# A gated linear-attention layer on one core: a new order at head and tail, gate's low part ahead of the masks, and a shorter reciprocal root with ScalarE's square

## What is computed

```python
xn = layernorm(x)                       # over the features, eps 1e-5
q, k, v = silu(xn @ Wq), silu(xn @ Wk), silu(xn @ Wv)
# per head, decay exp(ld): S_t = exp(ld) * S_{t-1} + k_t v_t^T ;  o_t = q_t S_t
gate = (xn @ Wg1) @ Wg2                 # 256 -> 16 -> 256
o = o * sigmoid(gate)
o = o * rsqrt(mean(o * o over the head's 16) + 1e-5) * norm_w
s = o @ Wo
g = silu(dequantised(fp8(xn * scale)) @ dequantised(fp8(W2 * scale1)))
out = x + s * g
```

## Time and profile before

| | us |
|---|---|
| median of 3 runs | 157.53 |
| lowest, highest | 156.8, 158.95 |
| the profiled execution's own time | 157.87 |
| its span, first to last instruction | 156.1 |
| busy in the span: PE, PEld, DVE, ACT, POOL | 131.1, 110.5, 109.1, 72.7, 73.2 |
| mean granted TensorE clock | 0.967 |

### The profile page before, as it was taken

How to read it: one execution, slowest core, us unless ns; L and a number is a source line. 1 busy time by engine, 2 the same in 40 slices (tenths; PEclk the granted TensorE clock), 3 DMA queues, 4 the chain that set the end, 5 groups by cost and what they waited for, 6 DMA issues and landing times.

```text
span 156.1 us, 7273 instructions
## 1 busy us (share of the span) xinstructions
PE 131.1 (84%) x3156; PEld 110.5 (71%) x3156; DVE 109.1 (70%) x302; ACT 72.7 (47%) x133; POOL 73.2 (47%) x112
## 2 busy tenths in 40 slices
PE   4987793793899997999799979897999798879781
PEld 4876692571798786779677967686878786668770
DVE  0766999654797589848984898289738961765854
ACT  3597570847466635573557355436541653001000
POOL 5758657594633366526652656166316630040030
PEclk9999999569689999999999999999999999999999
DMA  3988000000000000100100010000200020020003
GB/s 82 274 263 274 8 0 6 0 6 0 6 0 4 4 4 21 51 4 4 45 28 4 4 60 16 0 8 0 73 4 6 0 71 0 4 71 4 4 22 112
DMA packets 6847, 6.06 MB, mean 39 GB/s; under 512 B 1376, under 2 KB 6816, under 8 KB 6816
## 3 DMA queue, kind: packets, MB, share of 16 engines
q1 hardware_dynamic: 6816, 5.60, 11.3%
HBM read 3.50 MB, written 2.10 MB: 36 GB/s over the span
## 4 chain that ended last, share of the span: by engine, by line
PE 54%; DVE 26%; issue 10%; ACT 5%; DMA 2%; SPq 1%; DVEq 0%; ACTq 0%
PE b_q L1098 9%; PE b_o L1054 8%; PE b_o L1038 5%; PE b_v L917 3%; PE b_v L1104 3%; PE b_x L890 3%; DVE probs L641 3%; PE b_s L954 3%; PE b_k L980 3%; PE b_s L970 2%; DMA w_f<-in_L_attn_Wq_dram 2%; DVE b_x L688 2%; DVE b_x L686 2%; DVE sg L736 2%; PE b_v L920 2%
## 5 line engine op out<-in xcount | busy, mean ns | idle before, releaser
L333 POOL TENSOR_TENSOR e_sum<-e_y,e_magic 128x512 f32<-128x512 f32 x8 | 10.7, 1341 | 18.8 <-DVE e_magic L626 18.8
L674 DVE SCALAR_TENSOR_TENSOR og<-gate_tanh,b_o 128x512 f32<-128x512 f32 x8 | 5.5, 688 | 17.7 <-PE b_o L1054 17.7
L1054 PE MATMUL b_o<-probs,v_par 64*32 64x64 f32 x1024 | 15.9, 230 | 1.4 <-issue 1.4
L351 POOL TENSOR_TENSOR own_mid<-state_mid,head_parity 128x128 f32<-128x128 f32 x8 | 3.2, 401 | 26.8 <-DVE state_mid L654 22.5
L1054 PEld LDWEIGHTS b_o<-probs,v_par 64*32 64x32 f32 x1024 | 10.5, 110 | 7.1 <-issue 6.0
L341 POOL TENSOR_TENSOR qd<-q_silu,q_decay 128x512 f32<-128x512 f32 x8 | 10.3, 1293 | 9.8 <-ACT q_silu L468 9.8
L1098 PE MATMUL b_q<-wo_scaled,on 128*128 128x256 f32 x56 | 14.2, 394 | 0.8 <-DVE on L715 0.8
L369 POOL TENSOR_TENSOR y<-sg,x_sb 128x512 f32<-128x512 f32 x7 | 8.9, 1270 | 11.3 <-DVE sg L736 11.3
L917 PE MATMUL b_v<-w_hi,xT_hi 128*128 128x256 f32 x32 | 9.0, 302 | 5.2 <-DVE g1T L636 4.9
L468 ACT ACTIVATE q_silu<-b_q 128x512 f32<-128x512 f32 x8 | 4.8, 598 | 18.1 <-PE b_q L909 18.1
L1098 PEld LDWEIGHTS b_q<-wo_scaled,on 128*128 128x128 f32 x56 | 10.0, 189 | 2.7 <-DVE on L715 1.0
...
## 6 DMA issues: line engine op xcount, KB each, us to landing
...
```

The source lines that it names most:

```text
L333: g.tensor_tensor(e4_sum[:], e4_y[:, n % 2], e4_magic[:, n % 2], ALU.add).then_inc(s_e4sum, 1)
L674: v.scalar_tensor_tensor(out=og[:, n % 2], in0=gate_tanh[:, n % 2], scalar=1.0, in1=ps_o, op0=ALU.add, op1=ALU.mult).then_inc(s_og, 1)
L1054: mm = t.matmul(ps_o[32 * r:32 * r + 32, c, z:z + C], v_par[rows, u, blk:blk + 2 * E], probs[rows, r, s, i:i + C], start=(half == 0 and s ...
```

## The change

- **Loop.** `low_g1` comes ahead of the four masks.
- **Root.** A seed and Newton step with tuned constants (three operations), then a third-order step: two products and a last multiply on DVE and, between them, a square with a bias on ScalarE (`square_w`). `head_spread`'s factor takes up the constant 3/8. `square_w(n - 1)` stands on ScalarE ahead of `silu_q(n + 1)`.
- **Wg2.** The four loads go into a zeroed `wg2_f32` (they wait for the fill), and the stack is one cast and one multiply-add with a column that is -1 on the low rows and 0 elsewhere.
- **Head.** Wv is loaded ahead of the second x tiles; the first scale has its own semaphore. w_hi of Wq moves from ScalarE to DVE. GpSimd fills its constants ahead of the first `norm_factors`, does the second behind both selects of the decay mask, and `round_y(0)` ahead of `decay_q(0)` and the sum for W2. ScalarE scales y ahead of the second table load and finds the over-range values of step 0 earlier. DVE takes exponent and magic of step 0 ahead of the masks and the W2 steps behind them. TensorE transposes k of step 0 between the halves of v.
- **Tail.** DVE finishes the root of step 6 but for its pair before it gates step 7; four `keep_warm` calls ahead of the last o matmuls go, and others become fewer (14 to 12 at the start, 4 to 2 and 12 to 5 at the end).

```diff
@@ sync
             load_w(1, Wk)
+            sp.dma_start(scales[:, 0:1], scale.unsqueeze(0).broadcast_to([P, 1])).then_inc(s_scale[0], 16)
+            load_w(2, Wv)
             sp.dma_start(x_sb[:, x_tiles(1), :], x_v[:, x_tiles(1), :]).then_inc(s_x[1], 16)
-            load_w(2, Wv)
...
+            sp.wait_ge(s_pool, 15)
             for r in range(4):
                 sp.dma_start(wg2_f32[32 * r:32 * r + GR, :], Wg2).then_inc(s_wg2, 16)
@@ gpsimd
             pool.wait_ge(s_pool, 11)
-            norm_factors(0)
...
-            g.memset(wg2_stack[:].bitcast(F32), 0.0).then_inc(s_pool, 1)
+            g.memset(wg2_f32[:], 0.0).then_inc(s_pool, 1)
+            norm_factors(0)
+            g.memset(minus_53[:], -5.0 / 3.0)
+            g.memset(minus_third[:], 0.0).then_inc(s_pool, 1)
...
+            g.memset(minus_third[64:96], -1.0).then_inc(s_pool, 1)
...
-                if c == 0:
-                    pool.wait_ge(s_pool, 18)
-                    norm_factors(1)
-                    pool.wait_ge(s_shift, 2)
-            pool.wait_ge(s_pool, 19)
+            pool.wait_ge(s_pool, 21)
+            norm_factors(1)
             pool.wait_ge(s_dvec, 5)
             decay_k(0)
+            round_y(0)
+            decay_q(0)
             pool.wait_ge(s_w2q, 3)
             g.tensor_tensor(w2_m[:], w2_y[:], w2_f32[:], ALU.add).then_inc(s_w2sum, 1)
-            decay_q(0)
             norm_factors(2)
-            round_y(0)
@@ scalar
+            def square_w(n):
+                act.wait_ge(s_rs, RS_STEPS * n + 7)
+                a.activation(rs_half, rs_err, ACT.Square, bias=minus_53[:, 0:1]).then_inc(s_rs, 1)
...
-            high_w(0)
...
+            act.wait_ge(s_scale[0], 16)
+            scale_y(0)
             a.activation(table_load[:, 1:2], eps_col[:, 0:1], ACT.Silu)
             silu_k(0)
...
             normalise(1)
-            act.wait_ge(s_small, 32)
-            scale_y(0)
...
             silu_k(1)
+            find_over(0)
+            act.wait_ge(s_pool, 18)
+            silu_v(1)
             gate(0)
-            act.wait_ge(s_pool, 17)
-            silu_v(1)
+            high_g1(1)
             normalise(2)
-            high_g1(1)
-            find_over(0)
...
                 if nxt:
+                    square_w(n - 1)
                     silu_q(n + 1)
@@ vector
-            def root_step(n, m):
...
+            def root_cubic(n):
+                dve.wait_ge(s_rs, RS_STEPS * n + 5)
+                v.tensor_tensor(rs_half, rs_var, og_rs[:], ALU.mult).then_inc(s_rs, 1)
+                dve.wait_ge(s_rs, RS_STEPS * n + 6)
+                v.tensor_tensor(rs_err, rs_half, og_rs[:], ALU.mult).then_inc(s_rs, 1)
+                dve.wait_ge(s_rs, RS_STEPS * n + 8)
+                v.scalar_tensor_tensor(out=rs_full, in0=rs_half, scalar=20.0 / 9.0, in1=og_rs[:], op0=ALU.add, op1=ALU.mult).then_inc(s_rs, 1)
...
-            for r in (0, 1, 3):
-                rows = slice(32 * r, 32 * r + GR)
-                v.tensor_copy(wg2_stack[rows], wg2_f32[rows]).then_inc(s_g2w, 1)
...
+            v.tensor_copy(wg2_hi[:], wg2_f32[:]).then_inc(s_g2w, 1)
+            dve.wait_ge(s_g2w, 1)
+            v.scalar_tensor_tensor(out=wg2_stack[:], in0=wg2_hi[:].bitcast(F32), scalar=minus_third[:, 0:1], in1=wg2_f32[:],
+                                   op0=ALU.mult, op1=ALU.add).then_inc(s_g2w, 1)
...
                 rsqrt(n - 1)
-                mask(n, 2)
-                mask(n, 3)
                 low_g1(n + 1)
-                mask(n, 0)
-                mask(n, 1)
+                for r in (2, 3, 1, 0):
+                    mask(n, r)
                 head_norm(n - 1)
@@ tensor
             project_v(0, 0)
+            transpose_k(0)
             project_v(0, 1)
-            transpose_k(0)
...
             state_steps(n)
-            keep_warm(4, b_v)
             from_chunk(n, 0, 0)
...
```

More of the change, by code:

```diff
@@ L179, in layer_kernel @@
         s_ld = sem("log_decay_loaded")
-        s_small = sem("small_loaded")
+        s_scale = [sem(f"scale{n}_loaded") for n in range(2)]
         s_pool = sem("pool_constants")
@@ L186, in layer_kernel @@
         s_hsum = sem("head_sum_ready")
-        s_whi = sem("w_hi_ready")
+        s_whi = [sem(f"w{name}_hi_ready") for name in "qkv"]
         s_wlo = sem("w_lo_ready")
@@ L596, in _ @@
                     silu_ffn(n + 1)
+                if not nxt:
+                    square_w(n - 1)
                 square_o(n)
+            square_w(STEPS - 1)
         @block.vector
@@ L681, in root_seed @@
                 dve.wait_ge(s_rs, RS_STEPS * n + 1)
-                v.tensor_scalar(og_rs[:].bitcast(I32), rs_var.bitcast(I32), -0.5, float(0x5F3759DF), ALU.mult, ALU.add).then_inc(s_rs, 1)
-            def root_step(n, m):
-                dve.wait_ge(s_rs, RS_STEPS * n + 3 * m + 2)
-                v.scalar_tensor_tensor(out=rs_half, in0=og_rs[:], scalar=-0.5, in1=rs_var, op0=ALU.mult, op1=ALU.mult).then_inc(s_rs, 1)
-                dve.wait_ge(s_rs, RS_STEPS * n + 3 * m + 3)
+                v.tensor_scalar(og_rs[:].bitcast(I32), rs_var.bitcast(I32), -0.5, float(0x5F1FFFF9), ALU.mult, ALU.add).then_inc(s_rs, 1)
@@ L688, in root_step @@
+            def root_step(n):
+                dve.wait_ge(s_rs, RS_STEPS * n + 2)
+                v.scalar_tensor_tensor(out=rs_half, in0=og_rs[:], scalar=-0.703952253, in1=rs_var, op0=ALU.mult, op1=ALU.mult).then_inc(s_rs, 1)
+                dve.wait_ge(s_rs, RS_STEPS * n + 3)
                 v.tensor_tensor(rs_err, rs_half, og_rs[:], ALU.mult).then_inc(s_rs, 1)
[L689 to L690 removed]
+                dve.wait_ge(s_rs, RS_STEPS * n + 4)
+                v.scalar_tensor_tensor(out=og_rs[:], in0=rs_err, scalar=0.703952253 * 2.38924456, in1=og_rs[:],
@@ L706, in rsqrt @@
                 root_seed(n)
-                for m in range(3):
-                    root_step(n, m)
+                root_step(n)
+                root_cubic(n)
                 root_pair(n)
@@ L784, in _ @@
             v.tensor_copy(kT[:, 0], ps_kT).then_inc(s_kT, 1)
+            exponent(0)
+            magic(0)
             for half in range(KH):
@@ L820, in _ @@
             add_state_end(0)
+            low_g1(1)
+            put_nan(0)
             dve.wait_ge(s_w2sum, 1)
             v.scalar_tensor_tensor(out=w2_q[:], in0=w2_f32[:], scalar=-1.0, in1=w2_m[:], op0=ALU.mult, op1=ALU.add).then_inc(s_w2q, 1)
-            low_g1(1)
-            put_nan(0)
+            v.reciprocal(inv_scales[:], scales[:]).then_inc(s_dvec, 1)
+            dve.wait_ge(s_dvec, 6)
+            v.tensor_scalar(descale[:], inv_scales[:, 0:1], inv_scales[:, 1:2], None, ALU.mult).then_inc(s_dvec, 1)
             dve.wait_ge(s_w2q, 5)
@@ L1130, in _ @@
             state_steps(0)
[L1131 removed]
+            pe.wait_ge(s_g2w, 2)
             gate(0)
```

76 lines of the change are left out of this document (33 added, 43 removed).

## The result

| | before | after |
|---|---|---|
| median of the runs made together, us | 158.24 | 150.09 (149.64 to 151.12) |
| the profiled execution, and its span | 157.87, 156.1 | 149.64, 147.9 |
| busy PE, PEld, DVE, ACT, POOL | 131.1, 110.5, 109.1, 72.7, 73.2 | 125.7, 105.7, 104.2, 74.1, 73.9 |
| mean granted TensorE clock | 0.967 | 0.965 |

The ratio of after to before is 0.952, 95% interval 0.947 to 0.957: 4.8% faster, 8.2 us by the profiled executions, where 11.3 were forecast. The ratios here leave disturbed executions out, so a ratio and a quotient of medians can differ, and the profiled executions of experiments 4 (154.91) and 6 (152.72) are among those left out.

What follows compares the result with a forecast made beforehand. In the loop DVE bounds the stretch from product to gate's low part, TensorE the rest. Loop 4.9, head 4.5 and tail 1.9 make 11.3 off 157.87, giving 146.6, or 146.3 on the median's scale; range 142.2 to 150.5.

Steps and rivals of the forecast that it cites:

- Loop, -4.9: Loop: v projection's 0.98 us wait for gate's low part goes in five steps, 4.9 us; bounds 3.5 and 5.5.
- the cover is 0.5 us: Loop: masks end at 92.8, TensorE reaches the gate matmul at 93.3, so the root's saving gains nothing there.
- Rival 2: Loop: instruction supply becomes the next limit, half of 4.9 us stays, giving 148.8; chance 0.08.
- Head, -4.5: Head: earlier normalisation, transposes and Wg2 stack bring the first head sums earlier, 4.5 us; bounds -2.0 and -7.1.
- (a): Head: ScalarE's copy of Wq goes to DVE, so the first normalisation starts 1.0 us earlier.
- (a) to (c): Head: Wq's copy to DVE, Wv loaded and split earlier, k's transposes ahead of v's second half; together 2.0 us.
- (d): Head: DVE's stretch from low part to stack's end takes 2.0 to 3.3 against 6.1 us; gate about 22.5, -4.2.
- Rival 1: Head: GpSimd's order and port waits delay w2_fp8 and third normalisation; 2.0 of 4.5 us stays, 148.8; chance 0.13.
- Tail, -1.9: Tail: fewer fillers and a shorter last root in the closing chain save 1.9 us; bounds 1.2 and 2.8.
- (e): Tail: four keep-warm calls (1.16 us) ahead of the last o matmuls go, the instruction stall grows instead; 0.2 us left.
- (g): Tail: the last root is on the path in full, -0.5 us.
- (h): Tail: TensorE's 24 fillers become ten taking 1.2 us, ending before the root; 0.9 us, of which DVE's product takes 0.3 back.

Runs made afterwards that it cites:

- 4: The changed kernel with gate's low part behind the first two masks again, the new root kept; median 153.85, ratio 0.958.
- 6: The changed kernel with the old root (three Newton steps on DVE, no ScalarE square), the low part still ahead of the masks; median 151.63, ratio 0.955.
- 7: The kernel before with one edit, gate's low part ahead of the four masks; median 153.57, ratio 0.975.
- 2: The changed kernel with DVE's 1024-column lag product waiting until GpSimd's first shift is out; median 150.09, ratio 0.949.
- 3: The changed kernel with the second norm factors between GpSimd's two selects again and DVE's second statistics ahead of Wv's split; median 149.77, ratio 0.948.
- 8: The changed kernel with the edits of 1, 2, 3 and 5 together; median 148.46, ratio 0.940.
- 5: The changed kernel with filler matmuls in TensorE's three pauses of the head; median 147.79, ratio 0.935.
- 1: The changed kernel with the four keep-warm calls put back ahead of the last step's o matmuls; median 149.1, ratio 0.941.

## Why the prediction was right or wrong

The direction was right, the size wasn't: by the profiled executions 8.2 us came where 11.3 were forecast, and the median is 150.09, not 146.3.

- **Loop, -4.9: right, -5.5 measured.** No wait for the low part in any step, as shown by after and by 7, and it returns in 4. The square at 0.29 lies in "0.2 to 0.3", DVE's pause of 0.36 under 0.4, and q's silu is not held. Wrong was "the cover is 0.5 us": it is 0.2 with the new root and -0.2 with the old one (6), since TensorE's part of the step is 0.3 shorter without the wait. So the root is not worth nothing on the path but about 0.2 a step, and the loop gained 1.1 a step for the 0.98 counted. Rival 2, supply as the loop's next limit, did not come: the loop kept all of the gain.
- **Head, -4.5: the step that failed.** (a)'s "1.0 earlier" and "Together 2.0" for (a) to (c) were set without any wait between DVE and GpSimd. The text had the trap, with its rows and the right rule, but applied it to (d) alone ("I count one such wait for the stack and one in front of w2_fp8"). It holds as well for a 2-column GpSimd instruction beside DVE's product (2: 0.97 against 0.20), and for casts beside the selects (3: 1.12 and 1.50 against 0.39 and 0.71). That the second normalisation's factors "come out about where they were" and "have cover" was wrong too: in after they hold ScalarE for 1.77 before 16.00, behind statistics that wait for Wv's split. So TensorE came to the gate at 24.4 instead of 21.8 to 22.2, and the stack, whose multiply-add took 1.41, ended at 24.11 instead of 22.5. Three lone DVE instructions of over 1 us stand between 15 and 30, the sign the text named for "wrong". With both places mended and the clock full (8) the gate is at 22.98 and the first head sums at 35.53, against "near 22.5" and "near 35.3": but for these waits and the clock, the head's sum was sound.
- **The clock: named, priced too low.** "I expect that dip again, earlier, and no gain from it" was right for its place, and the sum needed no more. What the text missed is that it decides what a gain in the head is worth. Of the 0.7 to 1.2 that 2 and 3 win up to the head sums nothing can be told at the first projection; 5 wins 0.3 there and arrives 1.6 earlier; and with full clock in both, 1.47 of the 1.67 by which 8 leads 5 arrive. Rival 1 (only 2.0 of 4.5 stays) is what came, by port waits in places other than it named.
- **Tail, -1.9: -0.7 measured.** (e) was right: the stall grew by 0.8 for 1.16 of fillers. (g) and (h) were right: the root ends at 141.04+0.42 and the fillers at 141.3, just before it. Missing from the sum was the low clock over filler and head sums, about 1.2: ten passes took 2.50 instead of 1.38 (as in 1), and 3, with after's tail but no dip, has 22.95 for 24.19. "A low clock after 50 us" was named as a sign of being wrong, without a price. In sum 146.6+2.5 (head) -0.6 (loop) +1.2 (tail) = 149.7, the profiled 149.64.

Open: why a stall of 1.94 brought the dip in after and none in 3. The two differ in the time at which it falls (132.04 against 133.09) and in the stall ahead of it (0.41 against 0.68), and no run here varies one alone. Open too is why stalls 127 matmuls apart end 3.4 us apart in one kernel and 4.5 in another.
